# Two moves in a transformer-block kernel: the transposed-probability copies from ScalarE to VectorE, and a small table preparation from the second attention stage to the first layer-norm stage

## What is computed

```python
def attn(x, Wq, Wk, Wv, Wo):
    Q = x @ Wq; K = x @ Wk; V = x @ Wv            # one head, D_K = 128
    logits = einsum('bqd,bkd->bqk', Q, K) * d_k ** (-0.5)
    logits = where(causal, -inf, logits)
    return einsum('bqk,bkd->bqd', softmax(logits), V) @ Wo

def ffn(x, W1, b1, th, wr, wi, W2, b2):           # 1024 -> 4096 -> 1024
    hidden = einsum('bsd,df->bsf', x, W1) + b1
    imag = wi * sin(th + hidden * 0.1)
    phase = cos(th) * wr + sin(th) * wi
    return einsum('bsf,fd->bsd', relu(hidden + phase * imag * 0.1), W2) + b2

xn = layernorm(x)                                 # x: 16 x 2048 x 1024, float32
x = x + attn(xn, ...) + ffn(xn, ...)
```

## Time and profile before

| | us |
|---|---|
| device time, median of 2 runs | 1235.91 (1234.78 to 1237.04) |
| the profiled execution's own time | 1237.21 |
| its span on the slowest core (core 2), first to last instruction | 1235.6 |
| spans of the eight cores | 1225.5 to 1235.6 |
| busy on core 2: PE, ACT, DVE, POOL | 1082.8, 630.6, 404.4, 37.1 |

### The profile page before, as it was taken

The page is one execution under the profiler, slowest core; times in us unless marked ns, Lnnn a source line. Parts: engine busy times, 40 slices in busy tenths (PEclk is TensorE's granted clock), DMA queues, the critical chain, the costliest instruction groups (busy, mean ns, idle before and its releaser), DMA issues.

```text
span 1235.6 us, 23665 instructions; the slowest of 8 cores (1225.5 to 1235.6 us)
## 1 busy us (share of the span) xinstructions
PE 1082.8 (88%) x7810; PEld 744.2 (60%) x7936; DVE 404.4 (33%) x927; ACT 630.6 (51%) x1365; POOL 37.1 (3%) x48
## 2 busy tenths in 40 slices
PE   2756485669999999999999999999999999999998
PEld 1644374546666666566656665666566656665665
DVE  3511262203333333333333333333333333333333
ACT  2857586665444544454445454445454445444444
POOL 1310032000000000000000000000000000000000
PEclk9966686569999999999999999999999999999999
DMA  8789286931021020202020202020202020202010
GB/s 182 238 138 164 92 275 121 174 85 44 17 70 56 32 69 18 86 1 86 1 86 1 87 1 86 1 86 1 86 1 86 1 86 2 85 2 86 1 52 35
DMA packets 47415, 87.12 MB, mean 71 GB/s; under 512 B 7106, under 2 KB 23490, under 8 KB 46274
## 3 DMA queue, kind: packets, MB, share of 16 engines
q1 hardware_dynamic: 36226, 59.39, 15.1%
q0 software_dynamic: 11072, 26.22, 11.5%
HBM read 78.25 MB, written 25.17 MB: 84 GB/s over the span
## 4 chain that ended last, share of the span: by engine, by line
PE 72%; DVE 2%; issue 2%; DVEq 2%; ACT 1%; ACTq 0%
PE psOut L832 36%; PE psW L806 36%; DVEq L752 2%; DVE probs L754 1%; ACT rb_sb L779 1%; DVE u_sb L731 1%; DVE out_sb L754 0%; PE psOut L822 0%; DVEq L730 0%; DVEq L759 0%; DVEq L751 0%; DVEq L728 0%; ACTq L778 0%; ACTq L776 0%; ACT ss_sb L771 0%
## 5 line engine op out<-in xcount | busy, mean ns | idle before, releaser
L806 PE MATMUL psW<-xn_r,W_sb 128*128 128x256 bf16 x4096 | 538.3, 275 | 1.5 <-PEq L386 1.5
L832 PE MATMUL psOut<-W_sb,rb_sb 128*128 128x512 bf16 x1936 | 515.1, 383 | 17.0 <-ACT rb_sb L779 11.1
L806 PEld LDWEIGHTS psW<-xn_r,W_sb 128*128 128x128 bf16 x4096 | 404.5, 99 | 162.3 <-issue 5.6
L771 ACT ACTIVATE ss_sb<-psW,phb_sb 128x256 bf16<-128x256 f32 x512 | 242.1, 473 | 444.3 <-PE psW L806 444.0
L731 DVE SCALAR_TENSOR_TENSOR u_sb<-ss_sb,Rp_sb,psW 128x256 f32<-128x256 bf16 x512 | 244.3, 480 | 590.5 <-ACT ss_sb L771 577.6
L832 PEld LDWEIGHTS psOut<-W_sb,rb_sb 128*128 128x128 bf16 x2048 | 200.3, 98 | 151.5 <-issue 20.2
L779 ACT ACTIVATE rb_sb<-u_sb,b_sb 128x256 bf16<-128x256 f32 x511 | 254.4, 498 | 58.1 <-DVE u_sb L731 56.2
L526 PE MATMUL psT<-diag_li,xn_rg 128*128 128x128 bf16 x272 | 34.7, 283 | 27.1 <-ACT pT_big L644 25.7
L370 PE MATMUL psTx<-diag_li,probs 128*128 128x128 bf16 x176 | 15.1, 235 | 38.2 <-DVE diag_li L274 38.0
L540 PE MATMUL psO<-pT_big,V_tm 128*128 128x128 bf16 x272 | 32.1, 282 | 17.9 <-ACT pT_big L644 17.6
L526 PEld LDWEIGHTS psT<-diag_li,xn_rg 128*128 128x128 bf16 x272 | 25.6, 130 | 32.7 <-issue 32.0
(11 more groups left out here) (92 smaller groups left out, 441.9 us busy)
## 6 DMA issues: line engine op xcount, KB each, us to landing
x_sb<-x SPq DMA_DIRECT2D x52, 512.0 KB, 5.5
W_sb<-w POOLq DMA_DIRECT2D x8, 2048.0 KB, 39.8
xn_scr<-xn_rg POOLq DMA_DIRECT2D x32, 256.0 KB, 4.5
xn_r<-xn_scr SPq DMA_DIRECT2D x16, 512.0 KB, 6.9
out<-out_sb SPq DMA_DIRECT2D x32, 256.0 KB, 2.6
out<-probs SPq DMA_DIRECT2D x32, 256.0 KB, 4.8
xn_r<-x SPq DMA_DIRECT2D x12, 512.0 KB, 6.5
Q_fm<-b2rep SPq DMA_DIRECT2D x1, 512.0 KB, 3.4
```

What stands on the lines that cost most here:

```text
L771: ssc3.inc(sc.activation(ss_sb[ci % 2][:], psW1[slot][:], AF.Sin, scale=0.1, bias=phb_sb[:, c:c + 1]))
L806: ins = t.matmul(psW1[slot][:], W1_sb[:, k * DFF + c * 128: k * DFF + (c + 1) * 128], xn_r3[g % 2][:, k * R3:(k + 1) * R3], start=(k == 0) ...
L832: ins = t.matmul(psOut[tt][:, h * 512:(h + 1) * 512], rb_sb[cw % 3][:, tt * 128:(tt + 1) * 128], W2_sb[:, cc * D + h * 512: cc * D + (h + ...
```

## The change

There are two parts, and neither changes what is computed.

1. In both attention stages the copies `psT2` to `pT_big` leave ACT's program and stand in DVE's, behind the `diag_li` of the same tile, each with a `drain` ahead of it. The semaphores are the same.
2. The preparation, its DVE lists (`pv`) and its five ACT instructions, leaves the attention of sequence 1 and stands in the LN stage of sequence 0. There ACT's Sin, Sin and Square stand ahead of the loop, Sign ahead of round 12's Sqrt and Arctan ahead of round 14's. DVE's pieces stand at the end of rounds 0 to 9, 13 and 15, behind the `diag_li` of that round.

```diff
+                if s == 0:
+                    vops = [lambda v: v.wait_ge(sp1.h, 2)]
...
+                    for i, fn in enumerate(vops):
+                        pv.setdefault(min(i // 3, 9), []).append(fn)
...
                             sdg3.inc(ins)
+                        if j < NT1:
+                            for fn in pv.get(j, []):
+                                fn(v)
...
                     sc.wait_ge(sc0.h, 128)
+                    if s == 0:
+                        sc.activation(col(5), th_sb[:], AF.Sin, scale=1.0 / 16)
+                        sc.activation(col(4), th_sb[:], AF.Sin, scale=1.0 / 32)
+                        sc.drain()
+                        sp1.inc(sc.activation(col(6), col(4), AF.Square), 2)
                     for j in range(NT1 + 2):
                         jj = j - 1
+                        if s == 0 and j == 12:
+                            sc.wait_ge(sp2.h, 1)
+                            sc.drain()
+                            sp3.inc(sc.sign(col(7), col(1)))
+                        if s == 0 and j == 14:
+                            sc.wait_ge(sp2.h, 2)
+                            sc.drain()
+                            sp3.inc(sc.activation(col(6), col(5), AF.Arctan))
...
-                if s == 1:
-                    vops = [lambda v: v.wait_ge(sp1.h, 2)]
...
                         se2.inc(ins)
-                        for fn in pv.get(j, []):
-                            fn(v)
+                        for si in range(nsg[j]):
+                            b = bank_of[(j, si)]
+                            v.wait_ge(stx2.h, stx2_b + cum_sg[j] + si + 1)
+                            if j >= 1:
+                                v.wait_ge(spv.h, spv_b + j)
+                            v.drain()
+                            w = segw2(j, si)
+                            (st2e if b == 0 else st2eV).inc(v.tensor_copy(
+                                pT_big[si // 2][:, (si % 2) * 512:(si % 2) * 512 + w],
+                                psT2[b][:, 0:w]))
...
-                        if j >= 0:
-                            for si in range(nsg[j]):
-                                b = bank_of[(j, si)]
-                                sc.wait_ge(stx2.h, stx2_b + cum_sg[j] + si + 1)
-                                if j >= 1:
-                                    sc.wait_ge(spv.h, spv_b + j)
-                                w = segw2(j, si)
-                                (st2e if b == 0 else st2eV).inc(sc.copy(
-                                    pT_big[si // 2][:, (si % 2) * 512:(si % 2) * 512 + w],
-                                    psT2[b][:, 0:w]))
```

More of the change, by code:

```diff
@@ L249, in _, with _o, _mid, _tail @@
                     g.sem_inc(sbar.h, 1)
+                NF = NCF
+                col = lambda i: prep[:, i * NF:(i + 1) * NF]
+                pv = {}
+                if s == 0:
+                    vops = [lambda v: v.wait_ge(sp1.h, 2)]
+                    def _o(fn):
+                        vops.append(lambda v, fn=fn: (v.drain(), fn(v)))
+                    _o(lambda v: v.tensor_scalar(col(1), col(6), -2.0, 1.0,
+                                                 ALU.mult, ALU.add))
+                    _o(lambda v: v.tensor_copy(col(0), col(5)))
+                    for _ in range(4):
+                        _o(lambda v: v.scalar_tensor_tensor(col(2), col(0), 2.0,
+                                                            col(1), ALU.mult, ALU.mult))
+                        _o(lambda v: v.tensor_tensor(col(3), col(0), col(0), ALU.mult))
+                        _o(lambda v: v.tensor_scalar(col(1), col(3), -2.0, 1.0,
+                                                     ALU.mult, ALU.add))
+                        _o(lambda v: v.tensor_copy(col(0), col(2)))
+                    _o(lambda v: v.tensor_tensor(col(2), col(1), wr_sb[:], ALU.mult))
+                    _o(lambda v: v.tensor_tensor(col(3), col(0), wi_sb[:], ALU.mult))
+                    _o(lambda v: v.tensor_tensor(col(2), col(2), col(3), ALU.add))
+                    _o(lambda v: v.tensor_tensor(col(3), col(2), wi_sb[:], ALU.mult))
+                    _o(lambda v: v.tensor_scalar(col(4), col(1), -1.0, None, ALU.mult))
+                    _o(lambda v: v.tensor_tensor(col(4), col(1), col(4), ALU.max))
+                    _o(lambda v: v.tensor_scalar(col(4), col(4), 1.0, None, ALU.add))
+                    _o(lambda v: v.reciprocal(col(5), col(4)))
+                    _o(lambda v: sp2.inc(v.tensor_tensor(col(4), col(0), col(5),
+                                                         ALU.mult)))
+                    for i, fn in enumerate(vops):
+                        pv.setdefault(min(i // 3, 9), []).append(fn)
+                    def _mid(v):
+                        v.wait_ge(sp3.h, 1)
+                        v.drain()
+                        sp2.inc(v.tensor_tensor(col(5), col(4), col(7), ALU.mult))
+                    pv.setdefault(13, []).append(_mid)
+                    def _tail(v):
+                        v.wait_ge(sp3.h, 2)
+                        v.drain()
+                        v.scalar_tensor_tensor(Rp_sb[:], col(3), 0.1, col(7),
+                                               ALU.mult, ALU.mult)
+                        v.drain()
+                        v.tensor_scalar(col(5), col(6), 2.0, None, ALU.mult)
+                        v.drain()
+                        ins = v.scalar_tensor_tensor(phb_sb[:], b1_sb[:], 0.1,
+                                                     col(5), ALU.mult, ALU.add)
+                        sprep.inc(ins)
+                    pv.setdefault(15, []).append(_tail)
@@ L591, in _ @@
                     sc.wait_ge(sbar.h, bar_in)
-                    if s == 1:
-                        sc.wait_ge(sc0.h, 128)
-                        sc.activation(col(5), th_sb[:], AF.Sin, scale=1.0 / 16)
-                        sc.activation(col(4), th_sb[:], AF.Sin, scale=1.0 / 32)
-                        sc.drain()
-                        sp1.inc(sc.activation(col(6), col(4), AF.Square), 2)
                     for qq in range(NT1 + 1):
                         j = qq - 1
-                        if s == 1 and qq == 12:
-                            sc.wait_ge(sp2.h, 1)
-                            sc.drain()
-                            sp3.inc(sc.sign(col(7), col(1)))
-                        if s == 1 and qq == 14:
-                            sc.wait_ge(sp2.h, 2)
-                            sc.drain()
-                            sp3.inc(sc.activation(col(6), col(5), AF.Arctan))
                         if qq < NT1:
```

45 lines of the change are left out of this document (1 added, 44 removed).

## The result

The changed kernel takes 1227.1 us (the median of its runs), against 1235.3 for the kernel before on the same chips. The ratio is 0.9928 (95% interval 0.9916 to 0.9940), which makes the gain 8.9 us. The prediction said 1222, inside 1211 to 1232. Its sum had 14.3 us of gain, so 5.4 of them didn't come. Two of its terms are the main reason. In some executions (of the kernel before, too) one die is slower throughout at a lower granted clock: the ratios, and the time of experiment 10, leave these out, while the other times are medians of all executions and at most 0.7 us higher for it.

The account below looks back on a forecast made before the run. The feed-forward, PE busy 96%, stays unchanged; in the 275 us ahead no engine is full and PE and ACT take turns. Terms -7.0 - 10.9 + 3.6 = -14.3 gave 1222 us, range 1211 to 1232.

Parts of the forecast that it names:

- The forecast of -14.3: Whole kernel: -7.0 in the first attention, -10.9 in the second, +3.6 in the first LN stage; 1222 us, chance 0.65.
- one of being wrong: Signs against the forecast: DVE copies over 0.9 us, rounds keeping their length, feed-forward's own length moving, PE waiting for W2.
- Evictions to DVE, -7.0: Each attention: copies no longer queue behind ACT's exponentials; 7.0 us less, bounds -9.2 to 0.1.
- Rival C: Attention: moving evictions gives nothing, since PE and the next exponentials wait for the same chain; 1236 us, chance 0.12.
- The granted clock: Each attention: PE stands denser, so 0.9 us was allowed for a clock somewhat above 0.62.
- rival A: Attention: with PE's gaps shut the clock rises in half of the long rounds, 6.5 us more; 1213 us, chance 0.17.
- Preparation out of the second attention, -3.9: Second attention: 1.5 us less at its start, 2.35 at the Arctan; bounds -5.0 and -2.35.
- Preparation into the first LN stage, +3.6: First LN stage: DVE operations +1.4 us, Arctan with its loads +1.9, Sign +0.3; bounds 0.3 and 12.3.
- The Arctan's own term, +1.9: First LN stage: Arctan and two table loads take 2.94 us, partly absorbed by a 1.07 wait for PE; bounds 0 and 2.94.
- Sign's 0.3: First LN stage: ACT's Sign instruction adds 0.3 us.
- W2 has 13.6 us of room: Before the feed-forward: W2 lands at 261.6, feed-forward starts at 275.2, so the second attention's loss of 10.9 us fits.
- The table switch without a drain: First LN stage, Arctan: loads cost 1.28 us each without the skill's 1380 ns drain, which would add 2.8 for two switches.

Follow-up runs that it names:

- experiment 10: Changed kernel with DVE's preparation operations in rounds 3 to 11, Arctan at the first LN stage's end, W2's first eighth issued before attention 0; repeated run: 1217.4 us, ratio 0.9843.
- experiment 1: Kernel before with only the evictions moved to DVE, the preparation left in the second attention: 1231.0 us, ratio 0.9957.
- experiment 2: Changed kernel with the evictions back on ACT, so only the preparation is moved: 1235.9 us, ratio 1.0004.
- experiment 6: Changed kernel with the Arctan behind ACT's last transposed-tile copy of the first LN stage and `_tail` behind DVE's last round: 1223.0 us, ratio 0.9899.
- experiment 5: Changed kernel with DVE's small preparation operations in rounds 3 to 11 of the first LN stage instead of 0 to 9: 1224.8 us, ratio 0.9920.
- experiment 9: Changed kernel with DVE's preparation operations in rounds 3 to 11 and the Arctan at the first LN stage's end, W2 loaded whole in the second: 1220.6 us, ratio 0.9877.
- experiment 7: Changed kernel with DVE's preparation operations in rounds 3 to 11, Arctan at the first LN stage's end, W2's first eighth issued before attention 0: 1217.2 us, ratio 0.9860.
- Experiment 4: Changed kernel with Square in place of Arctan, taking away two table loads in the first LN stage: 1224.0 us, ratio 0.9910.

## Why the prediction was right, and where its terms were not

The number lies in the range, and the main step, that the copies' queueing behind exponentials costs time, is right. The forecast of -14.3 itself was 5.4 too much, and what the attention stages gave beyond their terms hid a part of what two other terms lacked. Of the signs that the prediction listed, one of being wrong came true, that PE stands waiting for W2. The attention stages came out under its 61 to 63 us, and the first LN stage over its 3 to 4 us of growth.

- **Evictions to DVE, -7.0.** Right in kind; the size came out in part by luck, as the next point shows. The 512-column copy took 0.692, from the row of 0.686; the first attention fell by 7.9 in the changed kernel, 8.1 in experiment 1, and by 5.6 in those runs where it was 61.3. Rival C, that all engines wait for one chain anyway, falls. Of the Trainium skill's two figures for this copy ("VectorE: DVE Perf Modes", section "The TRN2 errata"), the estimate of 0.66 was 0.03 too low: the row was the better source.
- **The granted clock.** I allowed 0.9 us for it, and gave rival A, a rise in half of the long rounds, 13.5 per attention in all. The clock did rise, from 0.62 and 0.59 of full speed to 0.76 in both stages. In the seven rounds from tile 8 to tile 14 of the first attention of core 4 it is 0.94, where the kernel before has 0.77:

```profile
98.13:135.44 37.31, 24.39 (x209) 17.35 (x210) 4.05 (x21) 27.48 (x59) 0.00 (x0) 0.77 0.68 112
```
```profile
106.61:136.67 30.06, 20.58 (x209) 13.79 (x210) 19.00 (x46) 16.50 (x36) 0.00 (x0) 0.94 0.85 149
```

  These rounds gave 7.3 us, 1.0 each, where I had 0.65. The rounds ahead of them gave 1.2 where I had about 2.1, and the last one cost 1.0 where I had 0.6. At the lower level tile 8's round gave 0.51 where my working had 0.67, and at the higher 1.40. So a part of rival A did happen, and the sum came out near -7.0 through smaller terms and a larger one. A's full price didn't come. One reason is in the windows: the kernel before already had 0.77 there and not the lower level alone. That the rounds at 1.00 hang on DVE's copies is likely but wasn't tested; PE waits 17 us for them in this stage on core 4, and 21 for ACT's copies in the kernel before.

- **Preparation out of the second attention, -3.9.** The start gave its 1.5 or more (second LN with its start, -2.5 and -1.6), and the whole of stage and start gave 12.7 against 10.9. Alone, in experiment 2, the preparation's removal gave 4.1. But the sum treated the two parts of the change as independent. They aren't: left there beside the evictions, the preparation costs 12.6 in that stage (71.4 against 58.8), not 3.9.
- **Preparation into the first LN stage, +3.6: this step failed.** It measured +6.5. By the table of copies 3.3 of that is DVE's, all of it ahead of tile 4's copy, where I took 1.4. I had the operations' price nearly right (0.26 each, and 0.8 to 1.2 for three in a round), and let gaps absorb them that DVE has only from the eighth tile on. The slower of DVE (1.86 a round, now 2.7 to 3.0) and ACT (2.1) sets the first rounds, and that changed over. The Arctan's own term, +1.9, was right: tile 12's copy comes 1.9 later, and the wait ahead of it, 0.6 to 1.1 on the eight cores before, is gone on all of them. Sign's 0.3 doesn't show. What I put at nothing is what the pause does to PE. The copies of tiles 14 and 15 come another 0.3 and 1.0 later, behind matmuls of PE at the lower clock level. Between the copies of tiles 13 and 14 the granted clock is 0.50 on seven cores of the changed kernel and 0.63 on the eighth; in the kernel before it is 0.50 to 0.55 on six, and in experiment 6 1.00 on five. Wherever it is 1.00 up to tile 15's copy, those two steps take 2.13 and 1.19, not 2.8 and 2.9. That PE's stops lower the clock fits all this and wasn't tested apart. Experiments 6 and 5 took back 3.6 and 2.9 of the 6.5, and experiment 9, with both edits, 6.1.
- **W2 has 13.6 us of room, "so 10.9 fits": this step failed too.** The room was read on one core. On the eight cores of the same execution it is 7.8 to 16.4. The least is on core 4, where the feed-forward starts at 269.8 and W2 had landed by 262.0 (issued at 196.9, 65.1 to land). And the stage and its start lost 12.7, not 10.9: even core 2, on which the room was read, waits 2.4 us in the changed kernel. PE waits for W2 on six of eight cores, up to 4.5 us, and experiments 9, 10 and 7 show what that is worth, 2 to 4 us.
- **The table switch without a drain.** "ScalarE: Activation LUTs", section "What ACT_TABLE_LOAD costs", of the Trainium skill would have put 1.38 more at each. The trace doesn't agree: the rows at 62.83 to 65.66 hold two loads of 1.28 and an operation of 0.23 in 2.83. Experiment 4 took 3.6 out of the stage with two loads gone. That is 1.0 more than the loads' own time, but the excess lies at the copies of tiles 14 and 15 and not at the loads, and it is under the 5.3 that two loads with drains would make by the page's figures, an estimate.
- **The sum.** -14.3, and 2.9 for the first LN stage, and 2 to 4 for W2, less 2.7 that the attention stages gave beyond their terms, makes -10 to -12, against 8.9 measured. The stage medians are of one execution each, and those two are 11.4 us apart (1237.2 and 1225.8): the one before is 2 us above the median of its kernel's runs, the changed one 1.3 below. That is enough to cover what is left. Also, the forecast's own bounds (-9.2 to -3 an attention, +1 to +7) add up to 1215 to 1233 and not to 1216 to 1231; nothing hangs on that.

## What to carry to other kernels

Where two parts of a change share an engine's queue, price the second in the presence of the first: a producer that was free on an idle engine (here `_mid`) becomes a 4 us wait as soon as the engine gets bulk work ahead of it. A wait takes in extra work put ahead of it (here 0.6 to 1.1 us), but the pause reaches the other engines too: ask what they do while this one is busy, and at what clock they go on (here 1.3 us more at the last two copies). Where the work can go *into* a wait with nothing behind it that others need, it is nearly free (the Arctan at the stage's end cost 0.2). Put small operations into the rounds in which the engine already waits for data. And read the room of a transfer on the core with the least of it, not on the core of the page.

## What the runs showed of the hardware that I had not expected

The first attention has no fixed length in one and the same kernel. With the evictions on DVE (ten kernels, 80 cores) it is 58.3 to 59.0 us on 24, 61.0 to 61.3 on 29, and between these on 27. With it goes the moment at which the granted clock rises. In windows of core 0, the changed kernel (59.0) and experiment 6 (61.2), from near the stage's start on, with the columns of the earlier trace rows:

```profile
91.00:106.00 15.00, 11.46 (x91) 7.69 (x89) 8.30 (x24) 7.19 (x18) 0.00 (x0) 0.66 1.00 160
106.00:121.00 15.00, 9.43 (x107) 6.53 (x108) 9.75 (x22) 8.81 (x19) 0.00 (x0) 1.00 1.02 172
```
```profile
91.00:106.00 15.00, 12.07 (x82) 8.34 (x82) 7.52 (x21) 7.23 (x17) 0.00 (x0) 0.50 1.01 164
106.00:121.00 15.00, 10.33 (x100) 7.28 (x102) 9.38 (x23) 7.43 (x17) 0.00 (x0) 0.84 1.03 174
```

In the first, 2.4 GHz is granted before 106; in the second, the whole first window stands at 1.2 GHz. Before the rise PE did the same kind of rounds in both. In the profiled executions of experiments 5 and 6, most cores have the longer form, in that of the changed kernel most the shorter, so a comparison of two single profiles can be off by 2.3 us in this stage without any edit to it. In experiment 5's profile the 2.9 us less of the first LN stage are met by 2.3 and 0.6 more in the two stages behind it. What decides the moment stays open.
